# A gated cross-attention and mixture-of-experts block: the order of the weights and rows at the start, a second turn bank, and the order of the first down rows

## The chip, the cores and the metric

One core of a Trainium2 chip runs the kernel. Its engines are TensorE (PE, matmuls), VectorE (DVE), ScalarE (ACT), GpSimd (POOL) and SyncE (SP, which here issues nearly all DMAs). The metric is the device time of one execution in microseconds (us), the median of several; lower is better.

## What is computed

The input is x, 16 sequences of 128 channels by 1024 positions, and a context of the same shape. In short:

```
x = x + tanh(g0) * xattn(layernorm(x), ctx, w)     # per sequence
x = x + tanh(g1) * ffn(layernorm(x))               # per row of 1024

xattn: three cosine similarities of neighbouring columns of ctx (left, self, right) weigh
       three shifted copies of the normalised x; then out = w_flat @ them   (128 x 384 by 384 x 1024)
ffn:   routing = sum of the two largest of x @ gate_w                        (8 experts)
       shared  = relu(x @ up_w) ** 2 @ down_w                                (1024 -> 2048 -> 1024)
       routed  = ((x @ fc1_w) @ expert_w) * routing @ fc2_w                  (1024 -> 512 -> 512 -> 1024)
       layernorm(shared + routed, gamma, beta)
```

All is float32 in memory. The large products are made from pairs of fp16 numbers (a value and the remainder of its rounding), so each product is three matmuls: high by high, high by low, low by high.

## The kernel before, in words

**Blocks.** Four sequences (512 rows) make a block, four blocks make the input. A block goes through `up_half(n)`: 20 tiles, 4 of fc1 and 16 of `up_w`, each 24 matmuls of 128x128 by 128x512 into one of four PSUM banks; then `down_half(n)`: for each of its four sequences (rows j = 0 to 3) the matmuls of `down_w` into psS (`shared`, 16 steps i of 6 matmuls) and those of the folded weight into psR (`routed`, 24 matmuls). During the down half of block n, `xattn(n + 1, j)` of the next block is put in (18 matmuls), so that block n + 1 is ready when it starts. `XATTN_AT` says after how many steps of `shared` this happens: 5 for j = 0, 0 for the others.

**Other engines in an up half** (`up_half` of ACT and DVE). For each up tile ACT takes the ReLU from PSUM, DVE squares it, ACT copies it to fp16, DVE takes the remainder. Between these stand the sums for the next block's similarities (`sums`, at the steps `SIM_T`; POOL makes their products in `products`), the statistics of x (`x_stats`, at `X_T`) and the cosines (`cosines`, at `COS_T`). SP loads the tiles of the paired weights four ahead.

**A down half.** DVE adds `xattn`'s result to x and takes the statistics (`combine`), `scale_bias` makes scale and bias of them from eight small operations, ACT normalises (`x1_normal`) and splits, SP turns the rows by a DMA. POOL weighs the next sequence (`weigh`); its pairs are made by ACT (`f_his`), DVE (`f_los`) and POOL (`f_lo`). ACT takes psS (`take_s`, counted by `s_evac`), for which the next row's matmuls wait; in its program this stands behind `f_his(m, j + 1)`. DVE adds psR (`take_r`), then follow layer norm, `finish` and the store.

**The first block is different**, since weights arrive raw. At the start, `expert_fc2(l)` multiplies expert_w by fc2_w (four parts of 16 instructions) into the folded weight w2. The first block's similarities go through DRAM (`store_sims`, `load_sims`: 1.5 MB for a sequence, broadcast to all partitions). Products of x and similarities are made by POOL (`weigh`, two of them) and DVE (`weigh_last`), multiplied in float32 (`xattn_first`), normalised, transposed by PE in halves (`turn_first(j, h)`, into one PSUM bank, `turn_bank`), and split by ACT and DVE (`first_xt_hi`, `first_xt_lo`). Each weight needs a scale from its norm: ACT squares it (`up_square`, `w2_squares`, the square in `DN_SQUARE`), PE adds over partitions (`norm_over_rows`), DVE makes a power of two (`norm_scale`). Then the weights are split into pairs: `tile_hi`, `tile_lo` for up (three ahead, the rest during the up half, then stored to DRAM for later blocks), `w2_split_hi`, `w2_split_lo` and POOL's `move_w2` for w2, `dn_split_hi` and `dn_lo` for down_w (from step 17 on, the pieces `DN_LATE` during the first row of the down half; those in `DN_POOL` have their remainder made by POOL). A piece c overwrites what piece c - 2 was read from, so it waits for that one.

Every engine runs its own program in order; the order around the change is written out by hand.

## Time and profile before

| | us |
|---|---|
| median of 3 runs (lowest, highest) | 1063.29 (1062.03, 1064.96) |
| profiled execution | 1060.95 |
| its span, first to last instruction | 1059.2 |

| engine | busy us | share of the span |
|---|---|---|
| PE | 961.1 | 91% |
| DVE | 518.8 | 49% |
| POOL | 337.5 | 32% |
| ACT | 323.4 | 31% |

The busy tenths in 40 equal slices show PE at 9 or more nearly everywhere but in the first 14 slices. The chain of work that ended last has 70% of its length on PE, 8% on DVE, 5% each on ACT and DMA. A timeline row gives start and duration in us, the engine, the line, the operation, what it writes and reads, and in brackets how long the engine was idle before it and which engine and line ended that. The name with a q (DVEq, ACTq) is an engine's sequencer, that is a wait for a signal behind an operation. Line 1373 is `expert_fc2`, 1250 `xattn_first`, 1260 `turn_first`, 1237 `xattn`, 1267 a tile, 1317 `shared`, 1327 `routed`, 1226 a norm over rows.

### The profile page before, as it was taken

Reading aid. Unit: us, or ns where it says so; the run is one execution under the profiler, and the core shown is the slowest. Engines: PE = TensorE matmul, PEld = TensorE weight load, DVE = VectorE, ACT = ScalarE, POOL = GpSimd, SP = SyncE. Lnnn points to the kernel's source line nnn. Section 1 sums busy time; section 2 is a strip of 40 time slices with the busy share of each in tenths; the row PEclk is TensorE's granted clock in tenths of the full one; section 3 lists DMA queues with packets and bytes.
Section 4 is the critical chain, followed back from the end, with each engine's and each line's share of the span. In section 5 each row is a group of like instructions: output and inputs, shape, how many; then the busy total and the mean of one; then the engine's idle time right before and its main releaser. Section 6 shows DMA issues by size and latency. Waiting matters only on the chain.

```text
span 1059.2 us, 12379 instructions
## 1 busy us (share of the span) xinstructions
PE 961.1 (91%) x4562; PEld 444.4 (42%) x4562; DVE 518.8 (49%) x840; ACT 323.4 (31%) x441; POOL 337.5 (32%) x159
## 2 busy tenths in 40 slices
PE   0978798698599999979999999979999999999996
PEld 0435543243244444434444444434444444444442
DVE  6473577547787324526677225516677212221112
ACT  2366656544333112212332112213232212210001
POOL 3430051145776243122256243123356120000110
PEclk9989898888799999999999999989999999999999
DMA  8894465521422344342231453232241433300001
GB/s 298 246 313 195 155 229 174 184 80 52 114 80 79 120 157 149 102 122 80 80 119 40 121 195 132 84 119 80 80 119 41 129 128 102 100 1 1 20 20 40
DMA packets 61985, 123.95 MB, mean 117 GB/s; under 512 B 35043, under 2 KB 35171, under 8 KB 60643
## 3 DMA queue, kind: packets, MB, share of 16 engines
q1 hardware_dynamic: 61346, 122.60, 36.2%
q8 instruction: 38, 0.62, 0.3%
q10 hardware_dynamic: 576, 0.53, 0.1%
q14 instruction: 25, 0.20, 0.1%
HBM read 97.75 MB, written 19.07 MB: 110 GB/s over the span
## 4 chain that ended last, share of the span: by engine, by line
PE 70%; DVE 8%; ACT 5%; DMA 5%; issue 4%; POOL 3%; SPq 2%; DVEq 2%; POOLq 1%; ACTq 1%
PE psS L1317 28%; PE psS L1267 16%; PE psR L1267 13%; PE psR L1327 7%; PE psP L1237 4%; DMA ring<-pair_scratch 1%; SPq L299 1%; ACT hid L752 1%; DMA sim_scratch<-simo 1%; POOL big L513 1%; DMA hid<-sim_scratch 1%; DMA g_col<-in_g_ffn 1%; PE psP L1250 1%; DVE s L890 1%; DVE sim_side L1076 1%
## 5 line engine op out<-in xcount | busy, mean ns | idle before, releaser
L1317 PE MATMUL psS<-big,hid 128*128 128x512 f16 x1536 | 334.8, 379 | 0.5 <-POOL big L513 0.5
L1317 PEld LDWEIGHTS psS<-big,hid 128*128 128x128 f16 x1536 | 149.9, 98 | 181.0 <-issue 0.9
L1267 PE MATMUL psS<-xT,ring 128*128 128x512 f16 (+1 forms) x912 | 199.2, 379 | 15.3 <-DMA ring<-pair_scratch 11.1
L1267 PE MATMUL psR<-xT,ring 128*128 128x512 f16 (+1 forms) x912 | 190.0, 368 | 0.0
L1267 PEld LDWEIGHTS psS<-xT,ring 128*128 128x128 f16 x912 | 91.5, 101 | 120.3 <-issue 25.3
L1267 PEld LDWEIGHTS psR<-xT,ring 128*128 128x128 f16 x912 | 89.2, 98 | 97.3
L500 POOL TENSOR_TENSOR y<-y,lgb 128x1024 f32<-128x1024 f32 x15 | 35.3, 2354 | 257.7 <-ACT y L651 257.7
L1327 PE MATMUL psR<-w,lgb 128*128 128x512 f16 x384 | 85.5, 379 | 0.0
L1013 DVE SCALAR_TENSOR_TENSOR y<-psR,rw,y 128x1024 f32<-128x1024 f32 x15 | 19.2, 1283 | 123.6 <-PE psR L1327 123.6
L471 POOL TENSOR_TENSOR sides<-scr 128x1024 f32<-128x1024 f32 x12 | 29.1, 2426 | 148.5 <-DMA scr<-in_ctx 148.5
L1085 DVE TENSOR_TENSOR hid<-sim_side,hid 128x512 f16<-128x512 f32 x64 | 48.0, 750 | 45.2 <-ACT hid L675 45.2
L1237 PE MATMUL psP<-u_buf,wx 128*128 128x512 f16 x216 | 52.9, 403 | 17.4 <-DVE u_buf L930 17.3
L490 POOL TENSOR_TENSOR ring<-f_buf,ring 128x1024 f32<-128x1024 f32 x18 | 39.0, 2169 | 90.7 <-ACT f_buf L619 63.1
L599 ACT ACTIVATE sd<-sd 128x1 f32<-128x1 f32 x44 | 8.9, 202 | 176.7 <-DVE sd L858 176.6
L1076 DVE SCALAR_TENSOR_TENSOR sim_side<-psS,sim_side 128x512 f32<-128x512 f32 x32 | 22.1, 690 | 81.4 <-ACT sim_side L673 81.3
L675 ACT ACTIVATE hid<-sim_side 128x512 f16<-128x512 f32 x64 | 40.3, 630 | 65.5 <-DVEq L1079 65.5
L1327 PEld LDWEIGHTS psR<-w,lgb 128*128 128x128 f16 x384 | 37.6, 98 | 45.3
L1076 DVE SCALAR_TENSOR_TENSOR sim_side<-psR,sim_side 128x512 f32<-128x512 f32 x32 | 22.1, 691 | 66.1 <-ACT sim_side L673 65.1
L658 ACT ACTIVATE y<-psS,coef 128x1024 f32<-128x1024 f32 x16 | 17.8, 1113 | 116.5 <-PE psS L1317 114.1
L673 ACT ACTIVATE sim_side<-psS 128x512 f32<-128x512 f32 x32 | 19.1, 596 | 93.3 <-PE psS L1267 92.3
L989 DVE TENSOR_TENSOR sides<-scr,sides 128x1024 f16<-128x1024 f32 x12 | 27.6, 2297 | 30.2 <-ACT sides L639 30.2
L1237 PEld LDWEIGHTS psP<-u_buf,wx 128*128 128x128 f16 x216 | 21.7, 102 | 47.5 <-issue 20.6
(189 smaller groups left out, 1058.3 us busy)
## 6 DMA issues: line engine op xcount, KB each, us to landing
ring<-pair_scratch SPq DMA_DIRECT2D x60, 512.0 KB, 3.5
ring<-sim_scratch SPq DMA_DIRECT2D x18, 504.0 KB
big<-in_w_up SPq DMA_DIRECT2D x8, 1024.0 KB, 14.7
out_rows<-y SPq DMA_DIRECT2D x15, 512.0 KB, 3.0
big<-in_w_down SPq DMA_DIRECT2D x14, 512.0 KB, 5.3
scr<-in_ctx SPq DMA_DIRECT2D x12, 576.0 KB, 4.0
pair_scratch<-ring SPq DMA_DIRECT2D x12, 512.0 KB, 5.8
sim_side<-sim_scratch SPq DMA_DIRECT2D x11, 504.0 KB
```

The lines of the kernel that those rows point to most:

```text
L471: pool.tensor_tensor(sides_a[:, :], scr_a[:, 0:T], scr_a[:, P:CTX], ALU.mult)
L490: pool.tensor_tensor(rows, f_b[b_of(m, j)][:, k:k + T], rows, ALU.mult).then_inc(t_rdy, 1)
L500: pool.tensor_tensor(y[:, :], y[:, :], gam, ALU.mult)
L675: act.activation(hT[:, t - LT, 0, :], buf, ACT.Copy).then_inc(h_hi, 1)
L989: dve.tensor_tensor(x_pair[:, :, 1, :], scr[0].rearrange("p (k i) -> p k i", k=KB), x_pair[:, :, 0, :], ALU.subtract).then_inc(xp_rdy, 1)
L1013: dve.scalar_tensor_tensor(out=y[:, :], in0=psR[:, :], scalar=rw[:, j:j + 1], in1=y[:, :], op0=ALU.mult, op1=ALU.add).then_inc(r_evac, 1)
L1076: dve.scalar_tensor_tensor(out=hbuf[:, t % 2, :], in0=bank, scalar=0.0, in1=hbuf[:, t % 2, :], op0=ALU.max, op1=ALU.mult)
L1085: dve.tensor_tensor(hT[:, t - LT, 1, :], hbuf[:, t % 2, :], hT[:, t - LT, 0, :], ALU.subtract).then_inc(h_rdy, 1)
L1237: mm = pe.matmul(psP[:, h, :], wx[:, k, w, :], U[b][:, k, v, HALF * h:HALF * h + HALF], start=(k == 0 and n == 0), stop=(k == G - 1 and n ...
L1267: mm = pe.matmul(up_bank[t % NR][:, cols], rows[:, a, k, :], xT[:, k, b, cols], start=(k == 0 and a == 0 and b == 0), stop=(k == KB - 1 an ...
L1317: mm = pe.matmul(psS[:, HALF * h:HALF * h + HALF], hT[:, i, a, P * j:P * j + P], dn[:, i, b, HALF * h:HALF * h + HALF], start=(i == 0 and ...
L1327: mm = pe.matmul(psR[:, HALF * h:HALF * h + HALF], lat[:, l, a, P * j:P * j + P], w2[:, l, b, HALF * h:HALF * h + HALF], start=(l == 0 and ...
```

## The change

**Start.** Expert and fc2 are loaded ahead of x. fc1 is loaded from ACT's queue, right after `norms(0)`, and no longer from SP's behind the similarity rows. Similarity rows get a third buffer, in `big`, and a semaphore for each sequence; three sequences' rows are asked for at once. The up loads are reordered: 0, 1, then 6 and 7 after `expert_fc2(3)`, then 2 and 3 once the third sequence is weighed, 4 and 5 behind one half of fc1's remainders each. The transposes of the two halves go to two banks, `turn_bank[0]` in psP and `turn_bank[1]` in psM. The orders on PE, ACT and DVE are rewritten to match.

**First up half.** ACT splits the next up tile between the ReLU and its copy to fp16, and DVE takes that remainder ahead of the other. The sums and cosines come one step later; the norm of down_w is summed one step earlier. The four w2 splits are spread over the steps 5, 6, 9 and 11, and POOL's copies over the products.

**All blocks.** `X_T` goes from 6 to 8; `combine` takes both halves of the statistics together; the two last operations of `scale_bias` are `tensor_scalar`.

**First down half.** Nine pieces of down_w instead of six are split before it, POOL makes four remainders instead of five; `xattn` comes after 8, 12, 10 and 6 steps; row 0 has `routed` behind `xattn`, ahead of the other half of `shared`.

```diff
-        S_first = ([sides_a[:, :], y[:, :], side_a[:, :]], [hid[:, (2 + k) * T:(3 + k) * T] for k in range(G)])
+        S_first = [[sides_a[:, :], y[:, :], side_a[:, :]], [hid[:, (2 + k) * T:(3 + k) * T] for k in range(G)],
+                   [big[:, (5 + k) * T:(6 + k) * T] for k in range(G)]]
-        turn_bank = psP[:, 2, :]
+        turn_bank = [psP[:, 2, :], psM[:, :]]
-        W2_SPLIT = {4: (0, 2), 5: (2, 4)}
+        W2_SPLIT = {5: (0, 1), 6: (1, 2), 9: (2, 3), 11: (3, 4)}
-        DN_SPLIT = {17: (0, 2), 18: (2, 4), 19: (4, 6)}
-        DN_LATE = range(6, IT)
-        DN_POOL = [c for c in range(IT) if c % 3 == 2]
+        DN_SPLIT = {17: (0, 3), 18: (3, 6), 19: (6, 9)}
+        DN_LATE = range(9, IT)
+        DN_POOL = [5, 8, 11, 14]
-        X_T = 6
-        XATTN_AT = (5, 0, 0, 0)
+        X_T = 8
+        XATTN_AT, XATTN_FIRST = (5, 0, 0, 0), (8, 12, 10, 6)
...
+            sp.dma_start(ET, w_expert).then_inc(e_in, 16)
+            sp.dma_start(fc2_raw, w_fc2.rearrange("(m p) h -> p m h", p=P)).then_inc(f2_in, 16)
             for j in range(BB):
                 sp.dma_start(home[:, j, :], x[j]).then_inc(x_first_in[j], 16)
...
-            for j in range(2):
+            for j in range(3):
                 load_sims(0, j)
-            sp.dma_start(fc1_flat, w_fc1.rearrange("p t k -> p (t k)")).then_inc(f1_in, 16)
             sp.wait_ge(t_rdy, G)
             sp.wait_ge(t_first, 1)
-            load_sims(0, 2)
-            load_up(0)
-            sp.wait_ge(t_rdy, 2 * G)
-            sp.wait_ge(t_first, 2)
             load_sims(0, 3)
-            for k in range(1, 4):
+            for k in range(2):
                 load_up(k)
-            sp.wait_ge(fc1_rdy, LT)
-            for k in range(4, 6):
-                load_up(k)
             sp.wait_ge(w2_done, LT)
             for k in range(6, 8):
                 load_up(k)
+            sp.wait_ge(t_rdy, 3 * G)
+            sp.wait_ge(t_first, 3)
+            for k in range(2, 4):
+                load_up(k)
+            for k in range(4, 6):
+                sp.wait_ge(fc1_rdy, 2 * (k - 3))
+                load_up(k)
...
                 for j in range(BB):
                     products(m, j)
-                    if first and j == 0:
-                        move_w2()
+                    if first:
+                        move_w2(*((0, 2), (2, 3), (3, 4), (4, 4))[j])
...
                         act.activation(buf, bank, ACT.Relu, scale=2.0 ** HID_SHIFT).then_inc(relu_rdy, 1)
-                        act.wait_ge(sq_hid, i + 1)
-                        act.activation(hT[:, t - LT, 0, :], buf, ACT.Copy).then_inc(h_hi, 1)
                     if first and EARLY + t < IT:
                         act.wait_ge(*out_of(t))
                         tile_hi(EARLY + t)
+                    if t >= LT:
+                        act.wait_ge(sq_hid, i + 1)
+                        act.activation(hT[:, t - LT, 0, :], hbuf[:, t % 2, :], ACT.Copy).then_inc(h_hi, 1)
...
             norms(0)
+            act.dma_start(fc1_flat, w_fc1.rearrange("p t k -> p (t k)")).then_inc(f1_in, 16)
...
-                dve.scalar_tensor_tensor(out=rsk[:, 0:1], in0=sdk[:, 2:3], scalar=scale,
-                                         in1=sdk[:, 3:4], op0=ALU.mult, op1=ALU.mult)
-                dve.drain()
-                dve.scalar_tensor_tensor(out=rsk[:, 1:2], in0=mvk[:, 0:1], scalar=-1.0,
-                                         in1=rsk[:, 0:1], op0=ALU.mult, op1=ALU.mult)
+                dve.tensor_scalar(rsk[:, 0:1], sdk[:, 2:3], sdk[:, 3:4], scale, ALU.mult, ALU.mult)
+                dve.drain()
+                dve.tensor_scalar(rsk[:, 1:2], mvk[:, 0:1], rsk[:, 0:1], -1.0, ALU.mult, ALU.mult)
...
-                        if t == SIM_T[j]:
+                        if t == SIM_T[j] + first:
                             sums(m, j)
+                    if first and EARLY + t < IT:
+                        tile_lo(EARLY + t)
...
-                    if first and t == SCALE_T:
+                    if first and t == SCALE_T - 1:
                         dve.wait_ge(dn_sq, IT)
                         norm_sum(WDN, LT, LT + IT)
+                    if first and t == SCALE_T:
                         norm_scale(WDN, 5)
...
                     if phase_a:
-                        done = XATTN_AT[j]
+                        done = (XATTN_FIRST if first else XATTN_AT)[j]
                         shared(j, 0, done, first and j == 0)
                         xattn(m, j)
+                    if first and j == 0:
+
+                        pe.wait_ge(up_evac, UT)
+                        routed(0, 0, LT).then_inc(r_done, 1)
...
             expert_fc2(0)
             expert_fc2(1)
             norm_over_rows(WX, 2, 1)
+            expert_fc2(2)
             xattn_first(0)
-            expert_fc2(2)
+            expert_fc2(3)
             norm_over_rows(WF1, 1, 2)
+            xattn_first(1)
             turn_first(0, 0)
-            xattn_first(1)
             turn_first(0, 1)
-            expert_fc2(3)
+            xattn_first(2)
             turn_first(1, 0)
-            xattn_first(2)
             turn_first(1, 1)
+            xattn_first(3)
```

Left out of this cut: ACT's order at the start (three of the `w2_squares` stand ahead of `f_rows(0, 3)`, the fourth behind the first transposes; four of the up squares there, then 12 to 15, 4 and 5, and the last six, 6 to 11, behind the last `first_xt_hi`), DVE's (each `weigh_last` behind the small scales, `fc1_los` in two halves, each ahead of a `combine`), and on PE the two first and two last half tiles, which stand together.

## Rows read from the trace of the kernel before

**Rows 1.** Busy time by stage: stretch, length, then each engine's busy us (count)

```profile
0.00:126.80 126.80, 83.75 (x344) 47.76 (x345) 65.75 (x132) 65.61 (x90) 30.78 (x25) 0.93 0.71 236
126.80:232.50 105.70, 90.64 (x450) 40.77 (x451) 67.68 (x90) 57.04 (x85) 34.95 (x17) 0.90 0.51 177
232.50:374.00 141.50, 124.24 (x559) 54.85 (x556) 96.60 (x130) 48.27 (x53) 81.33 (x37) 0.93 0.31 90
374.00:606.00 232.00, 226.01 (x1098) 102.68 (x1096) 120.14 (x195) 59.28 (x81) 84.75 (x36) 0.99 0.36 111
```

**Rows 2.** Waits of PE in the first 374 us: total, times, longest

```profile
PE psS L1373 <- DMA big<-in_w_fc: 25.5, 1, 25.5
PE psP L1237 <- DVE u_buf L930: 16.7, 2, 12.2
PE psP L1226 <- DVEq L1055: 10.7, 1, 10.7
...
PE psR L1267 <- DVEq L1078: 4.3, 1, 4.3
```

**Rows 3.** Chain of work, a full row of `shared`: start, duration

```profile
288.28 20.72 PE psS L1317 x96
```

**Rows 4.** Busy time by stretch in the opening; last are clock, DMA share, GB/s

```profile
10.00:15.00 5.00, 0.00 (x0) 0.00 (x0) 5.00 (x5) 2.33 (x2) 5.00 (x3) 1.00 1.02 417
...
26.00:28.00 2.00, 2.00 (x3) 0.68 (x2) 1.41 (x8) 0.20 (x1) 0.00 (x0) 1.00 0.00 0
```

**Rows 5.** Timeline of POOL in the opening, products of x and similarities

```profile
36.78 3.05 POOL L485 TENSOR_TENSOR u_buf<-f_buf,sim_side 128x1024 f32<-128x1024 f32 x1 [21.30 <-DMA sim_side<-sim_scratch]
...
44.69 5.35 POOL L485 TENSOR_TENSOR lgb<-hid 128x1024 f32<-128x1024 f32 x2 [2.55 <-DMA hid<-sim_scratch]
...
70.17 4.30 POOL L485 TENSOR_TENSOR lgb<-hid 128x1024 f32<-128x1024 f32 x2 [6.47 <-DMA hid<-sim_scratch]
```

**Rows 6.** Timeline of ACT in the opening

```profile
84.87 0.60 ACT L644 ACTIVATE xT<-psP 128x512 f16<-128x512 f32 x1 [4.24 <-PE psP L1260]
85.55 1.06 ACT L763 ACTIVATE work<-w 128x1024 bf16<-128x1024 f32 x1
```

**Rows 7.** Timeline of PE, norm of `up_w` and first up tiles

```profile
116.03 0.29 PE L1226 MATMUL psM<-nmx,ones_f 128*128 128x16 f32 x2
...
126.81 10.52 PE L1267 MATMUL psS<-xT,u_buf 128*128 128x512 f16 x48 [2.50 <-DVE lgb L1070]
```

**Rows 8.** Timeline of ACT and POOL in the first up half

```profile
171.68 0.60 ACT L673 ACTIVATE sim_side<-psS 128x512 f32<-128x512 f32 x1 [0.16 <-issue]
173.27 0.63 ACT L675 ACTIVATE hid<-sim_side 128x512 f16<-128x512 f32 x1 [0.99 <-DVEq L1079]
...
176.13 0.60 ACT L673 ACTIVATE sim_side<-psS 128x512 f32<-128x512 f32 x1 [0.15 <-issue]
...
209.45 0.60 ACT L673 ACTIVATE sim_side<-psS 128x512 f32<-128x512 f32 x1 [0.16 <-issue]
...
152.54 2.35 POOL L471 TENSOR_TENSOR sides<-scr 128x1024 f32<-128x1024 f32 x1
```

**Rows 9.** Timeline of ACT, DVE and PE in the first down half

```profile
238.45 2.17 ACT L711 ACTIVATE big<-big,wsc 128x1024 f16<-128x1024 f32 x2
...
260.13 3.06 DVE L1043 SCALAR_TENSOR_TENSOR big<-lgb,wsc,big 128x1024 f16<-128x1024 f32 x1 [1.28 <-ACT big L711]
...
272.17 2.21 DVE L872 SCALAR_TENSOR_TENSOR rs<-mv,rs 128x1 f32<-128x1 f32 x1
...
279.57 1.09 ACT L658 ACTIVATE y<-psS,coef 128x1024 f32<-128x1024 f32 x1
...
282.38 5.90 PE L1237 MATMUL psP<-u_buf,wx 128*128 128x512 f16 x18 [12.20 <-DVE u_buf L930]
```

**Rows 10.** Instructions of one line: duration in ns, least, median, greatest

```profile
L865 DVE TENSOR_SCALAR sd<-sd x44: 272/273/275, 56.8 to 1051.5; 128x1 f32<-128x1 f32 x44
...
L1000 DVE TENSOR_SCALAR amr<-amr x5: 153/154/1724, 46.0 to 213.3; 128x1 f32<-128x1 f32 x4, 128x2 f32<-128x2 f32 x1
```

113 lines of the change are left out of this document (54 added, 59 removed).

## Prediction

> **What bounds the kernel now.** I read the busy time by stage first [rows 1]. TensorE (PE) is the bound of the whole, but not evenly. A block at its natural pace is one `up_half` and one `down_half`; block 1 takes 232.0 us with PE busy for 226.0, and block 2 is like it. The first block takes 105.7 + 141.5 = 247.2 us with PE busy for 214.9, and ahead of it lie 126.8 us in which PE is busy for 83.8. The loss is in the first 374 us, and the change works there almost alone. Next, who PE waited for in those 374 us [rows 2]: the expert and fc2 weights (25.5), the paired rows of `xattn` in the first down half (16.7 in two waits, 12.2 the longer), the norm of `w_down` (10.7), an evacuation (4.3). 96 matmuls of this size take 20.72 us at full pace [rows 3], so 24 take 5.18, a tile of an up half; behind a long wait PE is slow for a while: 18 of them took 5.90 behind the wait of 12.2 [rows 9], where 3.9 is their share. The stages after 374 us are left as they are but for small things.
>
> **Opening, before: 126.8 us to the first tile of `up_w`.**
> (a) Expert and fc2 are ahead of x, so about 2.1 MB of x and 0.2 MB of small weights no longer lie in front of them. At 417 GB/s [rows 4] that is 5.6 us: PE starts at about 19.9 instead of 25.5 [rows 2]. x lands in time for its statistics, which vector work holds back today. By itself this gains little: the similarity rows pace what follows.
> (b) fc1 (2.1 MB) moves to ScalarE's (ACT's) DMA queue and starts at about 19. The DMA engines stand still around 26 to 28 us (0 GB/s) [rows 4], so it takes that gap and leaves the place between the second and third sequence's similarity rows. These rows come 7.9 us apart (POOL's products start at 36.78 and 44.69) when nothing lies between [rows 5]; four in a chain, which the third buffer permits, land at 36.8, 44.7, 52.6, 60.5. The last product of GpSimd (POOL) then ends at 60.5 + 5.4 = 65.9 instead of 74.5 [rows 5]: **8.6 us** earlier. SP's wait for the third sequence ahead of the up loads costs nothing as long as these land before ACT squares them: the last, issued near 79, lands near 84 at that rate and is squared after 95.
> (c) Behind that product ACT is the chain: 16 squares of up, 4 of the expert product, copies and normalisations. Three of the expert squares, 1.06 us each and some 0.2 to read out the sum [rows 6], move ahead into time in which ACT waits: **3.7 us**. The fourth stays.
> (d) With one turn bank, PE, ACT and VectorE (DVE) alternate, and ACT stood 4.24 us on a transpose that PE had queued behind an `xattn_first` [rows 6]. Two banks and the new order of PE take that and a little more: **4.5 us** (0 to 8). Six squares instead of two now stand behind the last copy, so PE, which could go on at 92, waits for the norm of `up_w` until about 99. I counted this: squares move, they don't vanish.
> From the norm to the tile after it, nothing changes: 126.81 - 116.03 = 10.8 [rows 7]. Sum: 8.6 + 3.7 + 4.5 = 16.8. A schedule laid out by hand, wait by wait, gives 109.8. Taken: **110.0, a gain of 16.8** (8 to 22).
>
> **First up half, before: 105.7 us.** A step of ACT is 4.45 us (171.68 to 176.13) [rows 8]; ahead of its copy to fp16, at 173.27, it stands 0.99 us while DVE squares [rows 8]. With the split of the next up tile in that gap, a step is about 3.4 us, well under PE's 5.18. But the extra work doesn't go: four sums of 2.6 us on DVE, four expert splits (each about 1 us on ACT and 1.3 on DVE), 16 squares of `w_down`, the statistics of x. And POOL computes the next sequence's products only after the copies of the expert halves in front: `move_w2(0, 2)` waits for the split of step 6, so the products that the sum of step 7 needs come some 4 us late, and again at step 10. Today POOL is held the same way (its product at 152.54 starts as the last copy ends) [rows 8]. I laid out steps 4 to 16: the ReLU of step 16 falls 79 us after the first up tile, against 82.6 today (209.45 - 126.81) [rows 7, 8], a gain of 3.5; and the sum for the norm moves a step earlier, 2.5 more. So PE's wait for the norm shrinks from 10.7 to no more than 8 to 10, and the 4.3 us wait to 2.3. **Gain 6.0** (0 to 15: if POOL's products cost nothing, PE waits for neither).
>
> **First down half, before: 141.5 us.** Four rows of 3.9 + 20.7 + 5.2 = 29.8 make 119 [rows 3]. The rest is a wait of 4.5 (16.7 - 12.2) at the first `xattn`, one of 12.2 at the second [rows 2], and slow matmuls behind them.
> (e) `XATTN_FIRST[0]` = 8 and `routed` behind it put 3 x 1.3 + 5.2 us of PE work ahead of where late pieces of `w_down` are needed; nine pieces instead of six are split before the stage. The 4.5 us become 1 or less, but by itself this only lengthens the next wait, since what PE waits for there is not PE's: nothing.
> (f) The second wait is put down to the pairs of sequence 1, whose `xattn` now comes after 12 steps. But PE also waits for `s_evac`, ACT's copy of psS, and this stands behind the same chain: it starts at 279.57 and ends at 280.7; PE goes on at 282.38 [rows 9]. So moving `xattn` doesn't remove the wait; it takes 1.7 us off. The chain starts when the last piece of `w_down` is done, at 260.13 + 3.06 = 263.2 or 30.7 us into the stage, and takes 17.5 us. Seven late pieces instead of ten, at today's pace of 2.5 us (from 238.5 on, 24.7 for ten [rows 9]), started 1 us later: done at 24.3 (22.5 by hand, wait by wait).
> (g) `scale_bias`: two `scalar_tensor_tensor` of one column become `tensor_scalar`. One of them took 2.21 us in this chain, beside a POOL operation [rows 9]. `tensor_scalar` with two column scalars takes 0.27 in each of 44 instances [rows 10]. So the chain shrinks by 1.9 to 15.6, and psS is free at 39.9 instead of 48.2; PE goes on at 40.4 instead of 49.9. **Gain 9.5** for the stage (4 to 14), (e) and (f) within it.
> The Trainium skill (SBUF — State Buffer, section Who interferes with whom) says that `tensor_scalar` can enter modes that take the port pair shared with GpSimd, and that whoever comes second is blocked. By that (g) would gain nothing and the sum would be 1.9 us less. The trace agrees only for two columns: L1000 took 1.72 us once, on 128x2, and 0.15 on 128x1, as L865 never waits in 44 [rows 10]; the new ones have one column.
> Then the rows 1 to 3. With `xattn` at step 12, its end to psS free is about 11 us (combination, statistics, normalisation, split, three copies, `take_s`), against 4 x 1.3 + 5.2 = 10.4 of PE work left: up to 1 us lost, 4 if POOL delays DVE. At steps 10 and 6 there is room.
>
> **The rest.** In the loop `x_stats` moves from step 6 to 8. Steps there take PE 5.18 and DVE some 3, so it is caught up before step 13: nothing. `combine` with its two statistics together costs up to 0.7 us where DVE waits for PE, saves a drain elsewhere: nothing. At the very end `scale_bias` costs 0.2.
>
> **Sum.** 16.8 + 6.0 + 9.5 - 0.2 = 32.1. The profiled execution took 1060.95 (its span and 1.75 around it), so 1028.9 in its terms; the median of the runs (1063.29) lies 2.3 above it: **1031**.
>
> **The rivals.**
> A, the opening gives half. fc1 on a second queue is served beside x and the first similarity rows, and the long chain of small waits in (d) holds: x is some 2 us later, each similarity row moves with it, (d) gives nothing. For it: DMA moves 417 GB/s ahead of that gap [rows 4], which is short of the 5.0 us that 2.1 MB take. Gain 16.8 - 8 = 8.8: 1039. The Trainium skill (DMA: Bandwidth & Descriptors, section Issuing engines are not separate DMA queues) says that transfers from several engines' queues share the same 16 engines and interleave, so the second queue gives no bandwidth, only the place in the order. By it x could lose up to the whole 5 us of fc1. 17%.
> B, the up half keeps up. POOL's products arrive in time and DVE reaches step 15 before PE ends tile 16. The stage is then 84.5 plus some 5: a gain of 16 instead of 6: 1021. 15%.
> C, psS in the rows behind. The chain behind the late `xattn` is held by POOL as today in each row (+4, +3, +2) and nothing of (g) comes: the down half gains 1 or so: 1040. 13%.
> D, slower. The weight stream becomes the bound. The loads of up tiles 8 to 11 stand in SP's queue behind two waits for `fc1_rdy`, and these behind two combinations and transposes on DVE; all stores of pairs and loads of `w_down` stand behind them. If the last load lands late, squares, norm and first tile follow one for one. I put it at 84, with 11 us of slack; slower than before by 0.3% needs 11 + 32 + 3 more, so it decides from 130 on. Against it: today all are loaded and squared by 116 [rows 7], and no wait in the chain ahead of them is that long. 1067. 3%.
> E, the order has no effect because some wait not seen here replaces all: 1062. 2%.
> The forecast with small shifts: 50%.
>
> **Numbers.** Low end: B with the down half at its best, 1031 - 10 - 5 = 1016. High end: A and C together, 1031 + 8 + 8.5 = 1048. Told apart from no change is about 0.3%. Faster: 0.95, same 0.02, slower 0.03.
>
> **What would show it.** First PE matmul at 20; POOL products in the opening starting near 37, 45, 53, 61; the norm of `up_w` at 99 and the tile after it at 110; the PE wait ahead of the norm of `w_down` still there and at most 9; the two of `scale_bias` at 0.27 or so each; in the down half one wait, between the first and the second row, of some 8 us, ended by ACT's `take_s` and no longer at `xattn`. Wrong if the opening ends after 118, if the third and fourth similarity rows are not 8 us apart, or if the loop blocks change by over 2 us.

## The result, and the profile after

The changed kernel takes 1048.41 us (median of 4, 1044.67 to 1050.65) where the kernel before takes 1064.03 on the same chip; the ratio is 0.985 (95% interval 0.982 to 0.989). The forecast was 1031 (1016 to 1048). The profiled execution took 1048.52, its span is 1046.7 (before 1059.2, or 12.5 more). Busy times of its page:

```profile
PE 957.6 (91%) x4562; PEld 443.2 (42%) x4562; DVE 476.7 (46%) x841; ACT 322.8 (31%) x441; POOL 336.9 (32%) x157
```

The stages, cut as in [rows 1]: opening, first up half, first down half, block 1 (stretch, length, busy us of PE, PEld, DVE, ACT, POOL, clock, DMA share, GB/s):

```profile
0.00:118.20 118.20, 82.19 (x344) 47.22 (x345) 59.31 (x132) 66.85 (x92) 30.79 (x25) 0.96 0.74 258
118.20:216.70 98.50, 87.00 (x451) 40.03 (x452) 71.84 (x87) 53.09 (x82) 32.02 (x15) 0.93 0.54 185
216.70:357.30 140.60, 125.17 (x559) 54.74 (x556) 78.99 (x135) 50.15 (x56) 79.37 (x36) 0.95 0.30 90
357.30:592.20 234.90, 227.15 (x1097) 102.90 (x1096) 109.53 (x195) 59.39 (x81) 87.25 (x36) 0.99 0.36 109
```

| stage | before | forecast gain | gain |
|---|---|---|---|
| opening | 126.8 | 16.8 | 8.6 |
| first up half | 105.7 | 6.0 | 7.2 |
| first down half | 141.4 | 9.5 | 0.8 |
| block 1 | 232.0 | 0 | -2.9 |
| block 2 | 234.1 | 0 | -1.3 |
| last block | 219.2 | -0.2 | 0.1 |

Three things need an explanation: half the gain of the opening, all of that of the first down half, and 4.2 us in the loop. The rows, in this order. DVE in the opening, its statistics of x:

```profile
28.92 1.29 DVE L958 BATCH_NORM_STATS2 st_x<-home 128x6 f32<-128x512 f32 x2 [3.50 <-DMA home<-in_x]
```

x is late now. POOL's products [rows 5]:

```profile
42.08 3.05 POOL L486 TENSOR_TENSOR u_buf<-f_buf,sim_side 128x1024 f32<-128x1024 f32 x1 [26.56 <-DMA sim_side<-sim_scratch]
...
48.68 5.36 POOL L486 TENSOR_TENSOR lgb<-hid 128x1024 f32<-128x1024 f32 x2 [1.25 <-DMA hid<-sim_scratch]
55.13 4.30 POOL L486 TENSOR_TENSOR u_buf<-f_buf,big 128x1024 f32<-128x1024 f32 x2 [1.09 <-DMA big<-sim_scratch]
67.01 3.04 POOL L486 TENSOR_TENSOR lgb<-hid,sim_side 128x1024 f32<-128x1024 f32 x1 [7.57 <-PE psP L1246]
70.02 2.34 POOL L486 TENSOR_TENSOR lgb<-hid,sides 128x1024 f32<-128x1024 f32 x1
```

The first is 5.3 us later than in [rows 5]; the next two follow 6.6 and 6.5 us apart; the fourth no longer waits for its rows but for an `xattn_first`, and the last ends at 72.4 (before 74.5). PE, norm of `up_w` and first up tile [rows 7]:

```profile
105.65 0.40 PE L1222 MATMUL psM<-nmx,ones_f 128*128 128x16 f32 x2 [3.63 <-ACTq L831]
...
118.21 5.99 PE L1265 MATMUL psS<-xT,u_buf 128*128 128x512 f16 x27 [2.51 <-DVE lgb L1065]
```

The first down half [rows 9]: DVE's first w_down differences and POOL beside them, the last late piece, the first `xattn`, `take_s`, and PE's second row (`shared` is L1315, `xattn` L1233 now):

```profile
208.11 9.52 DVE L1038 SCALAR_TENSOR_TENSOR big<-big,wsc 128x1024 f16<-128x1024 f32 x3 [0.35 <-ACT big L713]
...
209.92 3.34 POOL L491 TENSOR_TENSOR sides<-f_buf,sides 128x1024 f32<-128x1024 f32 x1
...
231.85 2.17 ACT L713 ACTIVATE big<-big,wsc 128x1024 f16<-128x1024 f32 x2
...
236.83 6.84 PE L1233 MATMUL psP<-u_buf,wx 128*128 128x512 f16 x18 [6.15 <-DVE u_buf L926]
...
243.80 1.15 ACT L713 ACTIVATE big<-big,wsc 128x1024 f16<-128x1024 f32 x1 [3.39 <-POOL big L514]
...
247.54 3.06 DVE L1038 SCALAR_TENSOR_TENSOR big<-lgb,wsc,big 128x1024 f16<-128x1024 f32 x1 [1.27 <-ACT big L713]
...
264.13 1.09 ACT L659 ACTIVATE y<-psS,coef 128x1024 f32<-128x1024 f32 x1
...
265.27 17.93 PE L1315 MATMUL psS<-big,hid 128*128 128x512 f16 x72 [6.07 <-ACT y L659]
```

The last piece of w_down is done at 250.6, 33.9 us into the stage; the forecast had 24.3, the kernel before 30.7. psS is free at 265.2, 48.5 us into the stage; forecast 39.9, before 48.2. PE also waits 6.15 us at the first `xattn`, where 1 or less was forecast and the kernel before had 4.5.

In the loop, PE's wait for tile 17 is 7.3 and 7.0 us (before 5.7 and 5.4). SP stores the similarities at the same 79.0 us into block 1 in both kernels, but asks for the rows 4.53 us later instead of 3.44, and the load of tile 17 stands behind. In that stretch the DMA queues show (packets, MB, share), first before, 452.9 to 456.3, then after, 436.3 to 440.8:

```profile
q1 hardware_dynamic: 1584, 0.05, 22.9%
```

```profile
q1 hardware_dynamic: 1584, 0.05, 18.2%
q8 instruction: 1, 0.02, 1.9%
q14 instruction: 1, 0.01, 0.8%
```

Two transfers of instructions lie in the store now.

### The profile page after: what moved, and what is told of

Read it like the earlier page. It is cut to its first block, busy times and chain, and to the rows that moved or that the text cites. A ratio compares the mean times of both kernels' runs of the same rounds, so it can differ in the third digit from the quotient of the medians.

```text
span 1046.7 us, 12359 instructions
## 1 busy us (share of the span) xinstructions
PE 957.6 (91%) x4562; PEld 443.2 (42%) x4562; DVE 476.7 (46%) x841; ACT 322.8 (31%) x441; POOL 336.9 (32%) x157
## 4 chain that ended last, share of the span: by engine, by line
PE 72%; DVE 6%; POOL 5%; DMA 5%; issue 4%; ACT 2%; POOLq 2%; DVEq 2%; SPq 1%; ACTq 0%
PE psS L1315 26%; PE psS L1265 16%; PE psR L1265 16%; PE psR L1325 7%; PE psP L1233 4%; PE psP L1246 2%; DMA ring<-pair_scratch 1%; DMA sim_scratch<-simo 1%; POOL ring L491 1%; DVE s L886 1%; DMA g_col<-in_g_ffn 1%; POOL big L514 1%; POOL home L580 1%; PE psR L1377 1%; DMA sim_side<-sim_scratch 1%
## 5 line engine op out<-in xcount | busy, mean ns | idle before, releaser
L1315 PE MATMUL psS<-big,hid 128*128 128x512 f16 x1536 | 337.9, 381 | 9.3 <-ACT y L659 6.3
L1315 PEld LDWEIGHTS psS<-big,hid 128*128 128x128 f16 x1536 | 150.1, 98 | 192.6 <-ACT y L659 7.3
L501 POOL TENSOR_TENSOR y<-y,lgb 128x1024 f32<-128x1024 f32 x15 | 39.2, 2613 | 255.0 <-ACT y L652 255.0
L1008 DVE SCALAR_TENSOR_TENSOR y<-psR,rw,y 128x1024 f32<-128x1024 f32 x15 | 19.2, 1281 | 140.1 <-PE psR L1325 140.1
L680 ACT ACTIVATE hid<-sim_side 128x512 f16<-128x512 f32 x64 | 40.2, 628 | 72.4 <-DVEq L1074 72.4
L659 ACT ACTIVATE y<-psS,coef 128x1024 f32<-128x1024 f32 x16 | 17.7, 1109 | 134.8 <-PE psS L1315 104.1
L1233 PE MATMUL psP<-u_buf,wx 128*128 128x512 f16 x216 | 51.4, 395 | 7.0 <-DVE u_buf L926 6.9
L503 POOL TENSOR_TENSOR y<-y,home 128x1024 f32<-128x1024 f32 x15 | 38.4, 2558 | 2.2
L674 ACT ACTIVATE sim_side<-psR 128x512 f32<-128x512 f32 x32 | 19.1, 596 | 64.5 <-PE psR L1265 63.3
## 6 DMA issues: line engine op xcount, KB each, us to landing
big<-in_w_up SPq DMA_DIRECT2D x8, 1024.0 KB, 11.1
```

The costliest lines, as they stand in the source:

```text
L501: pool.tensor_tensor(y[:, :], y[:, :], gam, ALU.mult)
L503: pool.tensor_tensor(y[:, :], y[:, :], home[:, j, :], ALU.add)
L674: act.activation(buf, bank, ACT.Relu, scale=2.0 ** HID_SHIFT).then_inc(relu_rdy, 1)
L680: act.activation(hT[:, t - LT, 0, :], hbuf[:, t % 2, :], ACT.Copy).then_inc(h_hi, 1)
L1233: mm = pe.matmul(psP[:, h, :], wx[:, k, w, :], U[b][:, k, v, HALF * h:HALF * h + HALF], start=(k == 0 and n == 0), stop=(k == G - 1 and n ...
L1315: mm = pe.matmul(psS[:, HALF * h:HALF * h + HALF], hT[:, i, a, P * j:P * j + P], dn[:, i, b, HALF * h:HALF * h + HALF], start=(i == 0 and ...
```

## The experiments

Every kernel is the changed one with the edit shown, but for the last but one. Lengths of the stages in their traces (op: opening, up 1, down 1: first halves), and medians. The medians come from several chips; each ratio is to the kernel before on the same chip.

| kernel | op | up 1 | down 1 | block 1 | block 2 | last | median | ratio to before (interval) |
|---|---|---|---|---|---|---|---|---|
| before | 126.8 | 105.7 | 141.4 | 232.0 | 234.1 | 219.2 | 1064.03 | |
| changed | 118.2 | 98.5 | 140.6 | 234.9 | 235.4 | 219.1 | 1048.41 | 0.985 (0.982-0.989) |
| e1_fc1_sp | 125.4 | 98.5 | 140.7 | 234.9 | 235.7 | 219.2 | 1056.00 | 0.993 (0.991-0.995) |
| e2_pe_order | 122.1 | 98.1 | 138.0 | 234.3 | 235.2 | 219.1 | 1050.87 | 0.989 (0.986-0.992) |
| e3_xt6 | 120.0 | 98.6 | 140.9 | 234.9 | 235.4 | 219.1 | 1049.21 | 0.986 (0.981-0.990) |
| e4_take_s | 119.7 | 98.6 | 137.6 | 234.2 | 235.8 | 219.1 | 1045.64 | 0.983 (0.980-0.987) |
| e5_sums_early | 117.5 | 98.2 | 140.1 | 235.1 | 235.4 | 219.0 | 1047.93 | 0.987 (0.983-0.991) |
| e6_fc1_mid | 115.0 | 99.0 | 140.6 | 235.4 | 235.4 | 219.3 | 1044.88 | 0.982 (0.977-0.986) |
| e7_expert_early | 115.6 | 98.7 | 140.8 | 234.5 | 235.3 | 219.1 | 1044.11 | 0.982 (0.978-0.986) |
| e8_down_old | 119.5 | 98.7 | 143.5 | 235.1 | 235.5 | 219.1 | 1053.06 | 0.990 (0.987-0.993) |
| e9_dn_vector | 118.0 | 98.5 | 130.4 | 234.3 | 236.0 | 219.1 | 1037.95 | 0.978 (0.975-0.980) |
| e10_pad_tensor | 120.2 | 98.4 | 140.9 | 234.2 | 233.0 | 219.1 | 1045.08 | 0.984 (0.982-0.987) |
| e11_pad_vector | 117.7 | 98.3 | 140.6 | 234.7 | 235.2 | 219.1 | 1046.17 | 0.985 (0.982-0.988) |
| e12_combined | 115.7 | 98.5 | 134.8 | 234.1 | 232.6 | 219.3 | 1037.26 | 0.978 (0.975-0.980) |
| e13_without_two | 114.1 | 98.8 | 131.0 | 234.6 | 232.8 | 219.2 | 1032.33 | 0.972 (0.969-0.974) |
| e14_before_vector | 127.4 | 105.5 | 131.6 | 234.0 | 235.2 | 219.2 | 1051.58 | 0.991 (0.988-0.993) |
| e15_old_scale_bias | 118.1 | 98.7 | 141.9 | 234.3 | 235.0 | 219.0 | 1048.32 | 0.986 (0.984-0.988) |

The opening, where nothing was changed in it, took 117.5 to 120.2 in nine traces: a difference of under 3 us there is no finding.

### The opening

**fc1 on SP's queue, behind three sequences' rows.**

```diff
-            act.dma_start(fc1_flat, w_fc1.rearrange("p t k -> p (t k)")).then_inc(f1_in, 16)
...
             for j in range(3):
                 load_sims(0, j)
+            sp.dma_start(fc1_flat, w_fc1.rearrange("p t k -> p (t k)")).then_inc(f1_in, 16)
```

> The changed kernel with fc1's load back on SP's queue, behind the three loads of similarity rows. Theory (fc1 on ScalarE's queue shares the DMA engines with x and with the store of the similarities): the DVE's wait of 3.50 us for x goes to under 0.5, the similarity store is issued near 26.5 instead of 31.5, the first POOL product starts near 37 to 38 instead of 42.1 and the second near 44. But fc1 then lands near 60 instead of near 30, and ScalarE's copy for the third product stands behind its square, so the fourth product ends no earlier than 72.3; first tile of up_w at 118 (within 3), time within 3 us of 1048. Rival (x is late for another cause: it now stands behind 2 MB of expert and fc2 weights): the wait for x stays at 3 to 3.5 us and the first product at 42.

DVE no longer waits for x, the rows are asked for 5.0 us after the store instead of 9.8, and POOL's first products start at

```profile
37.42 2.00 POOL L487 TENSOR_TENSOR u_buf<-f_buf,sim_side 128x1024 f32<-128x1024 f32 x1 [22.02 <-DMA sim_side<-sim_scratch]
...
44.46 5.36 POOL L487 TENSOR_TENSOR lgb<-hid 128x1024 f32<-128x1024 f32 x2 [2.42 <-DMA hid<-sim_scratch]
...
64.47 4.30 POOL L487 TENSOR_TENSOR u_buf<-f_buf,big 128x1024 f32<-128x1024 f32 x2 [14.66 <-ACT f_buf L617]
```

So fc1 made x and the first rows late. Where I was wrong is the whole: the third product waited 14.66 us for ACT, which stood before fc1's square, and the opening took 125.4 and not about 118. fc1 must come early, but not there.

**`xattn_first(1)` ahead of `expert_fc2(3)`.**

```diff
-            expert_fc2(3)
-            norm_over_rows(WF1, 1, 2)
             xattn_first(1)
+            expert_fc2(3)
+            norm_over_rows(WF1, 1, 2)
```

> The changed kernel with TensorE's first xattn product of sequence 1 ahead of the fourth expert product instead of behind it. Theory (the fourth POOL product, 67.0, waits for p_done of that xattn, which waits behind 6.9 us of expert product): xattn of sequence 1 starts near 55 instead of 61.4, the last POOL product starts near 61 to 62 instead of 67.0, the first tile of up_w is 3 to 5 us earlier (113 to 115), time 1044 to 1045. Rival (the chain behind it on ScalarE and VectorE holds the opening: copies, 16 squares): the product is earlier but the first tile of up_w stays within 1 us of 118.2, time 1048.

The last product starts at 61.5 as the theory says, but the tile comes at 122.1, later than either expected: fc1's norm now stands behind 7 us of expert product, DVE waits for it ahead of its second combination (70.4 instead of 68.1), and ACT's copies of fc1 follow. The product alone isn't the chain. (Its down half of 138.0, with nothing changed there, goes with a lighter overlap at the start: the three differences took 7.51 us, not 9.52, and the last piece is done 32.1 us into the stage, not 33.9.)

**fc1 between the first and the second rows.**

```diff
-            act.dma_start(fc1_flat, w_fc1.rearrange("p t k -> p (t k)")).then_inc(f1_in, 16)
...
-            for j in range(3):
+            load_sims(0, 0)
+            sp.dma_start(fc1_flat, w_fc1.rearrange("p t k -> p (t k)")).then_inc(f1_in, 16)
+            for j in (1, 2):
                 load_sims(0, j)
```

> The changed kernel with fc1's load on SP's queue between the similarity rows of the first and of the second sequence, instead of on ScalarE's queue beside x. Theory (beside x, fc1 delays x and the store of the similarities by 5 us, and these 5 us move the whole opening): the first product starts near 37.5 instead of 42.1, the second near 48.7 and the third near 55 as before; the first xattn is 4.5 us earlier and with it the combinations that follow; the first tile of up_w comes 2 to 4.5 us earlier, 114 to 116.5 (against 118.2 to 120.0 in the runs of the unchanged opening), time 1045. Rival (the second and third rows, not the first, hold the chain): the first tile stays at 118 to 120, time 1048.

DVE's eight statistics of x run without a wait, with expert and fc2 still ahead of x:

```profile
21.74 4.84 DVE L959 BATCH_NORM_STATS2 st_x<-home 128x6 f32<-128x512 f32 x8
```

The first product is at 37.1, the first tile at 115.0, 2.5 us ahead of the least of the nine.

**`expert_fc2(3)` and fc1's norm ahead of `xattn_first(0)`.**

```diff
-            xattn_first(0)
             expert_fc2(3)
             norm_over_rows(WF1, 1, 2)
+            xattn_first(0)
             xattn_first(1)
```

> The changed kernel with TensorE's fourth expert product and the norm of fc1 ahead of the first xattn instead of behind it: it fills part of the 4.9 us in which TensorE waits for POOL. Theory (the 7.0 us of expert product between the two xattn hold the second combination and the chain behind it): the first xattn starts near 49.6 instead of 47.5, the second near 58.5 instead of 61.4, the last POOL product near 64 instead of 67, the second combination near 64.5 instead of 68.1, the first tile of up_w 3 us earlier (115 to 117), time 1045.5. Rival (the delay of the first xattn by 2 us passes on to everything behind it): the first tile 1 to 2 us later, 1050.

The second xattn starts at 54.9 (changed 61.4), the second combination at 63.1 (68.1), the tile at 115.6, 1.9 us ahead of the least of the nine. So the order on PE also held the opening, about as much as fc1: the two medians, 1044.88 and 1044.11, lie 3.5 and 4.3 under the changed kernel's, on another chip. No run has both edits, so whether they add up is not shown.

### The first down half

**The down half's part undone.**

```diff
-        DN_SPLIT = {17: (0, 3), 18: (3, 6), 19: (6, 9)}
-        DN_LATE = range(9, IT)
-        DN_POOL = [5, 8, 11, 14]
+        DN_SPLIT = {17: (0, 2), 18: (2, 4), 19: (4, 6)}
+        DN_LATE = range(6, IT)
+        DN_POOL = [c for c in range(IT) if c % 3 == 2]
-        XATTN_AT, XATTN_FIRST = (5, 0, 0, 0), (8, 12, 10, 6)
+        XATTN_AT, XATTN_FIRST = (5, 0, 0, 0), (5, 0, 0, 0)
```

and `routed` of row 0 behind `shared`.

> The changed kernel with the first down half's part undone: two pieces of w_down a step are split ahead of it instead of three, ten late instead of seven, the xattn of the four rows after 5, 0, 0 and 0 steps, the routed product behind the shared ones. The new form of scale_bias stays. Theory (this part alone gives the stage next to nothing, since the wait for psS between first and second row takes its place): first down half 139 to 142 us against 140.6, with the wait of 4 to 6 us at the first xattn and one of 10 to 12 at the second; time within 2 us of 1048. Rival (the part is worth some 5 us but the earlier start of the stage has cost as much elsewhere): the stage takes 145 to 147, time 1053 to 1055.

The stage takes 143.5, between the two; the waits are nearly as expected, 14.1 us, the longer 9.7:

```profile
PE psP L1233 <- DVE u_buf L926: 14.1, 2, 9.7
```

The part is worth 2.9 us of the stage, not 9.5. (The median is 4.7 higher, but on another chip and with an opening of 119.5.) The other side of this run: its pieces and their order are those of the kernel before, yet the last is done 34.8 us into the stage instead of 30.7, and the stage takes 2.1 us more than the 141.4 of before, with the new `scale_bias` in it. By these two traces, what the change does ahead of the stage costs 2.1, and the two together make the 0.8. One thing differs there in the traces: POOL's products for the next block ended 9.4 us ahead of the stage, and now they run from 8.7 to 0.1 us ahead of it, beside the first differences.

**The sums one step earlier.**

```diff
-        W2_SPLIT = {5: (0, 1), 6: (1, 2), 9: (2, 3), 11: (3, 4)}
+        W2_SPLIT = {4: (0, 1), 5: (1, 2), 8: (2, 3), 10: (3, 4)}
-                        if t == SIM_T[j] + first:
+                        if t == SIM_T[j]:
```

and the cosines at `COS_T` in the first block too.

> The changed kernel with the splits of the expert weights one step earlier in the first up half and, as that permits, the sums and cosines of the next block at their old steps (one step, 5.2 us, earlier). Theory (in the changed kernel POOL's products for the next block, 208.0 to 216.5, fall on the first three w_down differences of VectorE, which take 3.2 us each instead of 1.28, and this crowds the start of the down half): the three differences take 1.3 us each, ahead of them or behind POOL, the second-to-last evacuation is not late, the last piece of w_down is done 29 to 30 us into the stage instead of 33.9, and the first down half shrinks by 2 to 4 us to 137 to 138.5; time near 1045. Rival (the late pieces are paced by their own chain, ScalarE to VectorE or POOL and back): the three differences are short again but the last piece is done at 33 us or later and the stage stays at 140.5.

POOL's products begin 10.3 us ahead of the stage instead of 8.7, not 5 earlier, so they still overlap; the three differences take 7.86 us. The last piece is done 33.0 us into the stage and the stage takes 140.1. The seven late pieces take 18.8 us, as without the edit, so this overlap isn't what paces them; but the edit was too weak to show what it costs.

**Differences on VectorE.**

```diff
-        DN_POOL = [5, 8, 11, 14]
+        DN_POOL = [15]
```

with POOL's piece in the down half.

> The changed kernel with fifteen of the sixteen w_down differences on VectorE (1.28 us each) and only the last on POOL, instead of four on POOL (1.12 + 2.12 us or more each). Theory (the sixteen pieces are one chain, ScalarE's copy of a piece waiting for the difference two pieces before it, and each POOL piece holds it by some 4.4 us; so the last piece is done 33.9 us into the stage however many stand ahead of it in the program): the seven late pieces take 10 to 12 us instead of 18.8, the last is done 24 to 27 us into the stage, TensorE's wait for psS shrinks from 6.1 to 0 to 3, the stage takes 133 to 137 instead of 140.6, time 1041 to 1045. Rival (the pieces are held by ScalarE's and VectorE's other work, the evacuations and the paired rows, and VectorE gets more to do): last piece at 32 to 35, stage 139 to 142, time 1047 to 1050.

```profile
231.20 2.17 ACT L710 ACTIVATE big<-big,wsc 128x1024 f16<-128x1024 f32 x2
235.82 2.34 ACT L710 ACTIVATE big<-big,wsc 128x1024 f16<-128x1024 f32 x2 [2.45 <-DVE big L1035]
...
240.77 1.28 DVE L1035 SCALAR_TENSOR_TENSOR big<-lgb,wsc,big 128x1024 f16<-128x1024 f32 x1
...
243.47 2.12 POOL L514 TENSOR_TENSOR big<-lgb,big 128x1024 f16<-128x1024 f32 x1 [0.15 <-issue]
...
257.08 15.71 PE L1312 MATMUL psS<-big,hid 128*128 128x512 f16 x72 [1.21 <-ACT y L656]
```

The six late pieces that are VectorE's take 10.9 us (231.20 to 242.05), to 25.6 us into the stage; in the changed kernel the seven, two of them POOL's, take 18.8 (231.85 to 250.60), to 33.9. The piece before the last, POOL's there, is done 7.3 us sooner in its stage. Where ACT waited 3.39 us for POOL it waits 0.2. The last one, POOL's here, is done only at 245.6, 29.1 us into the stage and later than the 24 to 27 expected, but the chain that frees psS goes on right behind VectorE's last piece, with statistics at 241.96, and doesn't wait for POOL's. The wait for psS is 1.21 instead of 6.07, that at the first `xattn` 3.2 instead of 6.15, and the stage takes 130.4, 10.2 less. Of this, 8.0 us are there when the second row starts; the other 2.2 are its first 72 matmuls, 15.71 us instead of 17.93: behind the wait of 6.07 PE's clock is granted at 0.87 over them, behind that of 1.21 at 1.00. The rival is out. The first three differences still took 9.27 us beside POOL.

**The same edit in the kernel before.**

```diff
-        DN_POOL = [c for c in range(IT) if c % 3 == 2]
-        DN_DVE = [c for c in range(IT) if c % 3 != 2]
+        DN_POOL = [15]
+        DN_DVE = [c for c in range(IT) if c not in DN_POOL]
```

> The kernel before, with fifteen of its sixteen w_down differences on VectorE and the last on POOL, nothing else. Theory (POOL's share paces the pieces, in this kernel as in the changed one): the last of the ten late pieces is done 24 to 26 us into the stage instead of 30.7, TensorE's wait between the first and second row shrinks from 12.2 to 5 to 7, the first down half takes 133 to 137 instead of 141.4, time 1054 to 1058. Rival (here the paired rows and the statistics that wait behind POOL hold the wait of 12.2): stage 139 to 142, time 1060 to 1064.

```profile
252.07 1.28 DVE L1040 SCALAR_TENSOR_TENSOR big<-lgb,wsc,big 128x1024 f16<-128x1024 f32 x1
...
254.61 2.12 POOL L513 TENSOR_TENSOR big<-lgb,big 128x1024 f16<-128x1024 f32 x1 [0.15 <-issue]
...
273.00 5.63 PE L1234 MATMUL psP<-u_buf,wx 128*128 128x512 f16 x18 [5.86 <-DVE u_buf L927]
```

VectorE's last piece is done at 253.35, 20.5 us into the stage (before 30.7), POOL's at 256.7, 23.8 into it; the wait of 12.2 is 5.86, and the stage takes 131.6, better than the theory's 133 to 137. This one edit gives the old kernel 9.8 us there; the whole reordering of the changed kernel gave 0.8.

**`take_s` of the first row ahead of the paired rows.**

```diff
                         x_hi(m, j)
+                        if first and j == 0:
+                            take_s(n, j, phase_a)
                         if j < BB - 1:
                             f_his(m, j + 1)
-                    take_s(n, j, phase_a)
+                    if not (first and j == 0):
+                        take_s(n, j, phase_a)
```

> The changed kernel with ScalarE's copy of psS, in the first down half's first row alone, moved ahead of the three copies for the next paired rows. Theory (TensorE waits for psS, and three copies of 1.1 us stand ahead of it): the wait of 6.07 us between the first and second row shrinks to about 2.8, nothing else becomes late (the paired rows are needed only after 12 steps), the first down half takes 137.3 instead of 140.6 us, time 1045. Rival (the rows after it are paced by the same chain): the xattn of the second row waits 3 us instead, the stage stays at 140.

The wait is 4.45 (2.8 was expected), the stage 137.6: a gain of 3.0, so the copies did stand in the way. The wait at the first `xattn` is 4.9 here and not 6.15; in `e6`, which has 4.9 there too, the wait for psS is 7.3 and the stage 140.6, so 2.8 of the wait go with the edit.

**The old `scale_bias`.**

```diff
-                dve.tensor_scalar(rsk[:, 0:1], sdk[:, 2:3], sdk[:, 3:4], scale, ALU.mult, ALU.mult)
+                dve.scalar_tensor_tensor(out=rsk[:, 0:1], in0=sdk[:, 2:3], scalar=scale,
+                                         in1=sdk[:, 3:4], op0=ALU.mult, op1=ALU.mult)
```

and the operation behind it likewise.

> The changed kernel with the two operations at the end of scale_bias as scalar_tensor_tensor again, as in the kernel before. Theory (they wait where POOL holds the port, 2.21 us once in the kernel before, and lie on the chain that frees psS): one or two of them in the first down half take 1 to 3 us, the wait of TensorE for psS behind the first row goes from 6.1 to 7.5 to 9, the stage from 140.6 (140.6 to 140.9 in four runs of this code) to 142 to 143; the rest within 0.5 us a stage; time 1050 to 1051. Rival (with the chain shifted they meet no POOL operation): stage 140.6 to 141, time 1048.

In the chain that frees psS, and at PE behind it:

```profile
256.66 1.17 DVE L867 SCALAR_TENSOR_TENSOR rs<-sd 128x1 f32<-128x1 f32 x1
257.92 2.21 DVE L870 SCALAR_TENSOR_TENSOR rs<-mv,rs 128x1 f32<-128x1 f32 x1
...
266.47 17.58 PE L1317 MATMUL psS<-big,hid 128*128 128x512 f16 x72 [9.56 <-ACT y L659]
```

The wait grows by 3.5 us, the stage by 1.3, and the median not at all (1048.32). But the stage began otherwise here: as in `e2`, the three differences took 7.51 us and the last piece is done 32.1 us into the stage. Beside `e2`, with a wait of 6.92 and a stage of 138.0, the old forms cost 2.6 us of the wait and 3.9 of the stage. The two operations themselves take 3.38 us in this chain, the new ones 0.42.

### The loop

**Statistics of x at step 6 in the loop.**

```diff
-                    if phase_a and t == X_T:
+                    if phase_a and t == (X_T if first else 6):
```

> The changed kernel with the statistics of x in the loop's up halves back at step 6 (in the first up half they stay at 8). Theory (the move to step 8 costs the loop blocks time): block 1 goes from 234.9 to about 232 us, block 2 from 235.4 to 234, the wait for tile 17's load from 7.3 and 7.0 to 5.5 us, time 1044. Rival (the move is free; the loop's length varies with when the DMAs land): blocks stay at 235, time 1048.

Blocks of 234.9 and 235.4, to a tenth those of the changed kernel: the step is free, as the rival has it.

**Code made longer, TensorE's.**

```diff
-            pe.wait_ge(const_rdy, 1)
+            for _ in range(49):
+                pe.wait_ge(const_rdy, 1)
             expert_fc2(0)
```

> The changed kernel with 48 more waits on an event long past at the very start of TensorE's program, 1.5 KB of code (time of its own: none, TensorE waits 19 us for data there). Both loop blocks of the changed kernel take 1.1 us more from the store of the similarities to the loads behind it (4.5 against 3.4), and in that store lie two transfers of instructions (at 437.2 and 437.6, store issued at 436.3), which in the kernel before were done ahead of it (451.8 and 452.6, store at 452.9). Theory (TensorE's fetch of instructions is one of them and delays the store): the fetch moves some 2.6 us ahead, off the store, the round trip goes back to 3.4 to 3.9, the wait for tile 17 from 7.3 and 7.0 to 5.5 to 6.5, the loop blocks from 234.9 and 235.4 to 232.5 to 234; time 1045 to 1047. Rival (the fetch doesn't move, or doesn't matter): round trip 4.1 to 4.8 and blocks of 235 as in every variant so far.

**Code made longer, VectorE's.**

```diff
+            for _ in range(11):
+                dve.drain()
             for j in range(BB):
                 sums(0, j)
```

> The changed kernel with 11 more drains at the start of VectorE's program, which makes its code as long as in the kernel before (time of its own: under 1 us, and VectorE waits there). Theory (the change shortened VectorE's code by 11 instructions, 704 bytes, which moved its fetch of instructions in the loop from just ahead of the store of the similarities into it): the second instruction queue's transfer moves back ahead of the store, the round trip to 3.4 to 3.9, the loop blocks to 232.5 to 234, time 1045 to 1047. Rival: as for the run before, nothing moves.

e10: waits for tile 17 of 6.21 and 5.90, blocks of 234.2 and 233.0; e11: 6.81 and 7.06, 234.7 and 235.2. With TensorE's padding the transfer of q8 is at 435.1, 3.4 us ahead of the store (438.4), and only this stays in the store:

```profile
q14 instruction: 1, 0.01, 1.0%
```

With VectorE's padding it is q14's that leaves (435.1, store at 435.9) and q8's that stays. The times from store to loads, blocks 1 and 2:

| transfers of instructions in the store | kernels | store to loads, us |
|---|---|---|
| none | before; e12; e13; e14 | 3.44, 3.34; 3.22, 3.38; 3.13, 3.35; 3.40, 3.15 |
| q14's | e10; e8 | 3.70, 3.72; 4.82, 4.35 |
| q8's | e11 | 3.99, 4.19 |
| both | changed; e9 | 4.53, 4.62; 4.07, 4.61 |

The other variants of the changed kernel without padding, `e8` aside, have both transfers there too and lie at 4.1 to 4.7. `e8` doesn't fit a count of transfers: q8's starts 0.9 us ahead of the store, q14's late in it, and yet it has 4.82, the longest time of all, and 4.35. So where in the store a transfer falls seems to matter as well; no run settles it. `e11` falls short of its theory, with blocks of 234.7 and 235.2 where 232.5 to 234 were expected; of `e10`'s, block 1 (234.2) is reached by `e4` without padding, and block 2 (233.0) by none (235.0 to 236.0). Each queue's transfer moved with its engine's code, so q8 carries TensorE's instructions and q14 VectorE's. The whole of the loop's loss isn't in it: from the load of tile 17 to its matmul it took 6.97 and 6.87 us before, 7.51 and 7.14 changed, and 6.83 to 7.87 in the variants and in e14. And `e14`, whose loop is that of before and whose stores are free of both, took 234.0 and 235.2 for the two blocks, 3.1 us more than the 232.0 and 234.1 of the kernel before; the trace of the kernel before, an execution of 1060.95 under a median of 1064.03, was a quick one. So most of the 4.2 us can be the difference between two traces of one loop.

### Together

**e12_combined**: the edits of e6, e9 and e4, both paddings (8 drains for VectorE), and, new:

```diff
-            weigh_last(3)
             combine(0, 1)
+            weigh_last(3)
             first_xt_lo(0, 0)
```

> The changed kernel with the edits that the runs so far speak for, together: fc1 between the first and the second similarity rows on SP's queue; VectorE's second combination ahead of its share of the fourth product, for which it waits until 65.2 in the run with fc1 there (new); fifteen of sixteen w_down differences on VectorE; ScalarE's first copy of psS ahead of the paired rows; both paddings of the code (48 waits for TensorE, 8 drains for VectorE, again 75,136 bytes). Theory (each cause is of its own and they add up): xattn of sequence 2 at 63.5 instead of 67.9, first tile of up_w at 111 to 113 (115.0 without the new edit), up half 98.5, first down half 129 to 130.4, round trips of 3.4 us and loop blocks of 232 to 233.5 (234.9 and 235.4), last stage 219.1: span 1024 to 1028, median 1026 to 1030. Rival (the causes hide one another: the up tiles' squares on ScalarE hold the opening at 115, and the down half's wait comes back in the second row): span 1032 to 1035, median 1033 to 1037.

The loop's theory holds for the round trips (3.22 and 3.38, waits of 6.4 and 6.1) and block 2 (232.6), not for block 1 (234.1), and the rest doesn't: opening 115.7, no better than `e6` alone (the second transposes waited 3.3 us for DVE instead), first down half 134.8 against 130.4 with `e9` alone.

**e13_without_two**: e12 without this edit and without e4's, both as in the changed kernel.

```diff
-            combine(0, 1)
             weigh_last(3)
+            combine(0, 1)
...
-                        if first and j == 0:
-                            take_s(n, j, phase_a)
...
```

> The combined kernel without two of its edits: ScalarE's copy of psS behind the paired rows again (it touches the first down half alone) and VectorE's second combination behind its share of the fourth product again (it touches the opening alone). Theory (with the last piece done at 25 us into the stage TensorE waits for its own row rather than for the chain, so the early copy gains nothing and delays the next paired rows): the first down half takes 130 to 131 instead of 134.8, with a wait of 1.2 us for psS behind the first row and at most 0.5 behind the second; opening 115 to 115.7; loop blocks 232.5 to 234; span 1029 to 1031, median 1030 to 1034. Rival (the 4.4 us were due to the clock or to when the stage begins): first down half at 133 to 135, span 1033 to 1036.

```profile
0.00:114.10 114.10, 81.32 (x344) 47.00 (x345) 63.67 (x132) 65.72 (x91) 31.05 (x25) 0.96 0.79 268
114.10:212.90 98.80, 87.44 (x448) 40.02 (x449) 72.21 (x87) 54.13 (x82) 32.02 (x15) 0.93 0.53 183
212.90:344.00 131.10, 122.46 (x561) 54.20 (x559) 76.68 (x138) 50.27 (x56) 67.85 (x30) 0.97 0.32 97
344.00:578.50 234.50, 227.52 (x1097) 102.97 (x1095) 109.66 (x196) 59.50 (x81) 87.53 (x36) 0.99 0.35 109
```

1032.33 us, a ratio of 0.972 (0.969 to 0.974), the best of these kernels and 16 us under the changed one's median; on another chip, so by the ratios it is 14. The early `take_s`, worth 3.0 us where PE waits for the chain, costs 3.8 where it doesn't: it delays the paired rows, and the wait behind the second row goes from 0.26 to 2.40.

## Why the forecast was wrong

**What bounds the kernel** was read rightly: all the gain is in the first 374 us.

**(a)** PE starts at 19.0 (forecast 19.9). "x lands in time" is false for the change as a whole, true for this step alone (e6).

**(b) failed, on two counts.** I took 0 GB/s from 26 to 28 us [rows 4] as the place that fc1 would fill. But it is issued at 18.6, while x and then the small store are still under way, and pushed both: 9.8 us from store to loads against 4.7 to 5.0 with fc1 elsewhere (e1, e6). The Trainium skill's rule (DMA: Bandwidth & Descriptors, section Issuing engines are not separate DMA queues) was weighed beside rival A, with "up to the whole 5 us of fc1" as its price; the runs show just these 5.0. And the pace of 7.9 us between rows was not one with nothing between: three rows at once come 6.5 apart, which gives 2.8 back over two gaps. Then the fourth product didn't wait for its rows at all but for `xattn_first(1)`, which the change itself put behind `expert_fc2(3)` (e7). The last product ended at 72.4, not 65.9.

**(c) and (d)** were right in their sum, and no run takes them apart: from the end of the last product to the norm of `up_w` it took 116.03 - 74.47 = 41.6 and now takes 105.65 - 72.36 = 33.3, a gain of 8.3 where 3.7 + 4.5 was forecast. Rival A had the opening's size (8.8, measured 8.6), but by luck: x and the rows were late as it says, yet (d) did give its share, and the wait for `xattn_first(1)` isn't in it. From norm to tile it took 12.6 instead of the unchanged 10.8: PE comes out of a wait of 3.63 and its clock is granted at 0.86 there, 1.00 before.

**Up half**: 7.2 instead of 6.0. The wait of 4.3 is gone; that for the norm is 11.5, not 8 to 10, since PE arrives sooner.

**(e) failed.** "The 4.5 us become 1 or less": they became 6.15. The pairs of the first row stand in ACT's program behind the pieces that are split ahead of the stage. With nine of these instead of six, ACT copies the pairs from 229.0 on, 12.3 us into the stage (before 235.61, or 3.1), and PE, which now arrives 14.0 us into it, starts `xattn` at 20.1 (before 11.1). I had moved PE's work in front of the wait and not looked at what the three more pieces stood in front of. Before, then changed:

```profile
235.61 1.04 ACT L627 ACTIVATE u_buf<-scr 128x1024 f16<-128x1024 f32 x1
...
243.60 6.52 PE L1237 MATMUL psP<-u_buf,wx 128*128 128x512 f16 x18 [4.46 <-DVE u_buf L930]
```

```profile
229.01 1.04 ACT L628 ACTIVATE u_buf<-scr 128x1024 f16<-128x1024 f32 x1
```

For the stage, the sequence together with the pieces is worth 2.9 (e8), not split further.

**(f) failed, and this is the largest miss.** I counted the late pieces from the stage's border: seven at 2.5 us, begun 7.0 us into it. But the border is a place in PE's program. The sixteen pieces are one chain that begins when the norm of w_down is known; calling nine of them early doesn't make them sooner. It begins 9.8 us ahead of the stage in both kernels. They began at 206.9 and ended at 250.6, 2.7 us each (before some 2.5), and the seven late ones began 15.2 us into the stage, not 7.0. I used the pace as given and didn't ask what set it; [rows 9] had only its sum. A piece waits for the difference of the piece two before it, and POOL needs 1.12 + 2.12 us or more for one where DVE needs 1.28. With POOL's share gone, VectorE is through 8.3 us sooner (e9), and it is so in the kernel before as well (10.2 sooner, e14). A term for the change's own cost was missing too: beside POOL's products, now later, the first three differences take 9.52 us, and `e8` puts what happens ahead of the stage at 2.1 us of it. Forecast, 24.3 + 15.6 = 39.9 us until psS is free; measured, 33.9 + 14.6 = 48.5: the start of the chain was wrong by 9.6 us, the chain behind it by 1.0 to the good.

**(g)** was right in kind and too small: 1.9 us forecast, while the two operations take 3.0 less (3.38 to 0.42, e15), and the stage 1.3 less, or 3.9 beside the trace that began alike (e2). The new forms take 0.21 us in each of 44:

```profile
L867 DVE TENSOR_SCALAR rs<-sd x44: 212/214/215, 58.4 to 1039.8; 128x1 f32<-128x1 f32 x44
```

The port rule of the Trainium skill (SBUF — State Buffer, section Who interferes with whom), weighed against it, doesn't bite on one column. For the old forms the trace agrees with what the same section says of VectorE instructions with two SBUF inputs: they meet POOL's. They took 1.17 and 2.21 us beside its products in `e15`, and 0.16 each at 251.7, where POOL stood still.

Rival C had the down half's size ("gains 1 or so", measured 0.8) and not the cause, which is luck again: behind the second row PE waited 0.26 us, and (g) came in full.

**The rest**: `X_T` is free, as said (e3). The loop's loss of 4.2 us had no term and no rival: 1.1 and 1.3 us of it are the round trip of the store, which the length of two engines' code moves. How much of it is a loss at all stays open, since `e14` shows 3.1 us between two traces of the same loop.

**The sum**: 32.1 forecast; 8.6 + 7.2 + 0.8 - 2.9 - 1.3 + 0.1 = 12.5 measured between the spans (15.6 between the medians, since the trace of the kernel before is a quick one). 8.2 of the missing are the opening, 8.7 the down half, 4.2 the loop; 1.2 came more in the up half and 0.3 at the end. The signs that I gave were the right ones: opening past 118, rows not 8 us apart, loop blocks off by more than 2.

## What to carry to other kernels

A chain of pieces isn't made earlier by moving its pieces across a border of the program: find what starts it and what sets its pace, and ask for the pace of each engine that takes part. A gap in the DMA engines' time is free only for a transfer that starts in it; one that is issued earlier on another queue is served beside whatever is under way (here fc1, issued at 18.6 us for a gap at 26, cost the rows 5.0). A wait that stands in for another is worth an edit only as long as it is the last to end: the same early copy gained 3.0 us in one kernel and lost 3.8 in the next.

## What was unexpected of the hardware

The engines' instructions come through the same DMA engines (in the page of the changed kernel 38 transfers of q8 with 0.62 MB, 24 of q14 with 0.20), and where such a transfer falls into a small, scattered store (1584 packets, 48 KB) on which a chain waits, it took 3.1 to 3.4 us from store to loads without one, 3.7 to 4.8 with one, 4.1 to 4.7 with both. 48 more waits at the start of TensorE's program move one of them out, 11 more drains in VectorE's the other. Why q8's transfer lies 2.3 us later in block 1 of the changed kernel (80.3 us into the block, before 78.1) stays open.

Beside POOL's products the w_down differences of DVE took some 3.1 us each in the changed kernel and in `e9` (9.52 and 9.27 for three) instead of 1.28, and POOL's products 3.34 instead of 2.35. No run took this overlap away; in `e2` and `e15` it was lighter (7.51) with nothing changed that bears on it, and the last piece was 1.8 us sooner.
